# Codebook and quantisation in one block, two thresholds per product over stacked half rows, keys' low parts by a product in the turned keys' bank

## What is computed

```python
lora_delta = lora_B @ lora_A * 0.5                       # 512x64 @ 64x512
cb = codebook / max(max|codebook|, 1e-8)                 # 64 entries, in any order
scale = exp(scale_log)                                   # one per row and group of 128
normalized = (weight + lora_delta) / scale               # 512 x 512
thresholds = (cb[:-1] + cb[1:]) * 0.5                    # 63
idx = searchsorted(thresholds, normalized, side='left')
w = (cb[idx] - normalized) + normalized
w_eff = w * scale + lora_delta
x = x + x @ w_eff.T
```

```python
x = x + attention(x, Wq, Wk, Wv, Wo, norms, k_cache, v_cache, block_table, cache_seqlens)
```

## Time and profile before

| | us |
|---|---|
| median of 3 runs (2248.16 to 2250.21) | 2248.35 |
| the profiled execution | 2244.9 |
| its span in the trace | 2243.0 |

### The profile page before, as it was taken

One profiled execution on the slowest core, in us unless ns is written; L12 is line 12 of the kernel. 1 busy time (PEld: TensorE's weight loads), 2 busy tenths in 40 slices (PEclk: granted clock), 3 DMA queues, 4 the chain that ended last, 5 costly groups with the idle time before them and its releaser, 6 DMA issues.

```text
span 2243.0 us, 61281 instructions
## 1 busy us (share of the span) xinstructions
PE 2158.3 (96%) x18068; PEld 1411.6 (63%) x18068; DVE 1727.7 (77%) x3942; ACT 1465.5 (65%) x4967; POOL 1251.3 (56%) x2067
## 2 busy tenths in 40 slices
PE   5786989999999999999999999999999999999998
PEld 2343556666666666666666666666666666666665
DVE  6995668777777777777777777777777777777785
ACT  2542557676677776676676667667666666666664
POOL 3422126656666655665656666666656566665663
PEclk9997999999999999999999999999999999999999
DMA  3687658667667667667669667666566656666663
GB/s 103 221 279 248 222 167 238 195 193 207 200 194 207 197 191 216 203 198 211 198 191 300 179 189 238 185 177 175 175 188 181 181 173 186 183 178 177 184 178 104
DMA packets 478727, 438.06 MB, mean 195 GB/s; under 512 B 53037, under 2 KB 407676, under 8 KB 477886
## 3 DMA queue, kind: packets, MB, share of 16 engines
q1 hardware_dynamic: 433278, 295.70, 44.7%
q0 software_dynamic: 40960, 134.25, 19.6%
q10 hardware_dynamic: 4160, 4.19, 0.5%
HBM read 377.24 MB, written 56.70 MB: 193 GB/s over the span
## 4 chain that ended last, share of the span: by engine, by line
PE 84%; DVE 1%; issue 0%; ACT 0%; DVEq 0%; ACTq 0%
PE PR L1257 21%; PE Op L1238 15%; PE WOp L1296 15%; PE Sp L1204 15%; PE PTp L1215 11%; PE TRp L1270 3%; PE Sp L1207 1%; PE Op L1220 1%; PE Op L1240 1%; PE TRp L1281 1%; DVE masked L1448 0%; PE WOp L1281 0%; ACT masked L1353 0%; DVE WoT L1507 0%; DVE OT L1466 0%
## 5 line engine op out<-in xcount | busy, mean ns | idle before, releaser
L669 POOL DMA_INDIRECT pages<-values_split,rows x512 | 526.4, 1028 | 104.0 <-issue 78.5
L1347 ACT ACTIVATE pts<-PTp 128x512 f16<-128x512 f32 x512 | 305.7, 597 | 363.9 <-PE PTp L1215 363.8
L1257 PE MATMUL PR<-Wt,xT 128*128 128x512 f16 x2232 | 539.1, 380 | 0.0
L1238 PEld LDWEIGHTS Op<-pts,pages 128*128 128x128 f16 x6144 | 385.4, 98 | 121.1 <-DVE OT L1466 4.2
L1238 PE MATMUL Op<-pts,pages 128*128 128x128 f16 x6144 | 426.6, 219 | 2.4 <-DVE OT L1466 2.3
L1204 PE MATMUL Sp<-pages,qT 128*128 128x512 f16 x1536 | 416.2, 380 | 6.9 <-PEq L184 6.9
L1448 DVE CUSTOM_DVE_ANT_0 masked<-Sp,mask 128x544 f32<-128x544 f32 x512 | 370.0, 723 | 60.4 <-PE Sp L1207 54.3
L1453 DVE TENSOR_TENSOR pts<-PTp,pts 128x512 f16<-128x512 f32 x512 | 351.5, 686 | 75.1 <-ACT pts L1347 74.9
L1353 ACT ACTIVATE masked<-masked,small 128x544 f32<-128x544 f32 x512 | 379.0, 740 | 9.4 <-DVE small L1448 8.5
L1296 PE MATMUL WOp<-WoT,OT 128*128 128x512 f16 x1536 | 377.5, 379 | 0.0
L1466 DVE TENSOR_TENSOR OT<-Op,OT 128x128 f16<-128x128 f32 x512 | 148.2, 289 | 266.3 <-ACT p L1341 262.7
(11 more groups left out here) (211 smaller groups left out, 3075.5 us busy)
## 6 DMA issues: line engine op xcount, KB each, us to landing
pages<-keys_transposed SPq DMA_DIRECT2D x2048, 64.0 KB
mask<-mask_rows SPq DMA_DIRECT2D x128, 128.0 KB
v<-new_values SPq DMA_DIRECT2D x96, 128.0 KB
weights_split<-wdst SPq DMA_DIRECT2D x40, 256.0 KB
keys_transposed<-pages SPq DMA_DIRECT2D x32, 256.0 KB, 3.4
values_split<-pages SPq DMA_DIRECT2D x16, 512.0 KB, 3.6
rope_s<-rope_table SPq DMA_DIRECT2D x32, 256.0 KB
pages<-values_split,rows POOLq DMA_INDIRECT x512
```

The lines of the kernel that those rows point to most:

```text
L669: nc.gpsimd.indirect_dma_start(out=vS[:, n % 2, c, :, :].rearrange("p l n -> p (l n)"), out_offset=None, in_=v_d, in_offset=bass.IndirectO ...
L1238: nc.tensor.matmul(o, vS[:, par, c, low, h * D:(h + 1) * D], pts[:, u % 2, part, c * P:(c + 1) * P], start=(k == 0), stop=False)
L1257: m = nc.tensor.matmul(bank(k), xT[:, c, xl, :], Wp[:, c, wl, GROUP_COL[k]:GROUP_COL[k] + HID], start=(i == 0), stop=(i == NPASS - 1))
L1347: nc.scalar.activation(pts[:, u % 2, 0, :], PTp[:, :], ACT.Copy).then_inc(G.pt_hi, 1)
```

## The change

The codebook block is gone as a block of its own; its work stands at the head of block 2, without a barrier behind it.

- **Order of SP's loads:** codebook, LoRA factors, scale_log, weight, then the first chunk of keys and values, the small tables, chunk 1; then the jump's store and load; then chunk 2 and the page table (`bt_raw`, formerly ahead of the small tables).
- **LoRA:** ScalarE, not VectorE, copies the turned lora_B and the four products. Sum and scaling of `norm` run in quarters of 512 columns.
- **Two thresholds per product:** ScalarE's queue copies rows 0 to 63 of `norm` by two DMAs (512 KB each) into the lower and upper 64 partitions of `pair_rows[0]`, and rows 64 to 127 likewise into `pair_rows[1]`. A comparison (`thr2`) tests 64 rows against an even threshold in partitions 0 to 63 and against the next, odd one in partitions 64 to 127. The weights of a product (`pair_weights`, 32 kept matrices) have 64 columns with the jumps' f16 parts and 64 with their low parts; both thresholds' contributions add up in the product. 64 comparisons (32 per half of the rows) and four f16 products for each.
- **Joining:** after each half ScalarE copies the four banks to SBUF (`sums_out`), high sums in partitions 0 to 63, low sums in 64 to 127; at the end two f32 products per bank with shifted identities (`joined`) add high and low and put both halves of the rows in place.
- **Keys' low parts:** the turned keys stay in their PSUM bank, a product of a negative identity with the f16 high part is added onto them (`rest`), and ScalarE copies the remainder (`keys_low`). The keys' staging has four buffers instead of two. Turns, copies and low parts have new places in the order of steps.
- **GpSimd:** `positions` come before the page table, which is worked through in two parts of 512 numbers after the values' chunks 3 and 8. **Angles:** four steps before the first comparison, four after steps 1 to 7; tables after steps 38 to 52.

The diff, cut to its core:

```diff
+        stacked = sb("stacked", [P, 3 * P // 2], F32)
+        thr2, jump2, jump2_lo = (scr[:, 3264 + 32 * i:3296 + 32 * i] for i in range(3))
+        pair_rows = [acc, wgt]
-        clear()
-        DRING, AHEAD = 8, 5
+        NP = NCB // 2
+        STEPS = 2 * NP
+        RING, AHEAD = 3, 5
...
@ sync
                 load(1)
+                sp.wait_ge(G.sq_done, 1)
+                sp.dma_start(jump_d[0:NCB - 1].rearrange("(n o) -> n o", o=1), tiny[0:63, 8:9]).then_inc(G.jump_moved, 16)
+                sp.wait_ge(G.jump_moved, 16)
+                sp.dma_start(jump[:, 0:NCB - 1], jump_d[0:NCB - 1].rearrange("(o n) -> o n", o=1).to_broadcast([P, NCB - 1])).then_inc(G.jump_moved, 16)
                 load(2)
+                sp.dma_start(bt_raw, page_list.to_broadcast([P, B * NPP])).then_inc(G.pages_loaded, 16)
...
@ tensor
+                def rest(n):
+                    pe.wait_ge(G.kt_hi, n + 1)
+                    nc.tensor.matmul(t_bank[n % 3].rearrange("p (h q n) -> p h q n", h=KVH, q=PPC), negident,
+                                     kst[n % 4][:, :, :, 0, :].rearrange("p q h n -> p h q n"), start=False, stop=True, skip_group_check=True).then_inc(G.kt_rest, 1)
...
+                turn(0)
+                turn(1)
+                turn(2)
+                pe.wait_ge(G.const_done, 3)
+                rest(0)
+                for step in range(STEPS):
+                    phase, j = divmod(step, NP)
+                    pe.wait_ge(G.mask16_done, step + 1)
+                    pe.wait_ge(G.diag_done, 2 * (j + 1) if phase == 0 else 2 * NP)
+                    for k in range(4):
+                        if phase == 1 and j == 0:
+                            pe.wait_ge(G.sums_out, k + 1)
+                        m = nc.tensor.matmul(q_bank[k], pair_weights[j], mask16[step % RING][:, k * 512:(k + 1) * 512], start=(j == 0), stop=(j == NP - 1))
...
+                    if step % 2 == 0 and step // 2 + 1 < NI:
+                        rest(step // 2 + 1)
+                    if step % 2 == 1 and step // 2 + 3 < NI:
+                        turn(step // 2 + 3)
+                for k in range(4):
+                    pe.wait_ge(G.sums_out, 4 + k + 1)
+                    nc.tensor.matmul(q_bank[k], joined[0], sums[0][k], start=True, stop=False)
+                    nc.tensor.matmul(q_bank[k], joined[1], sums[1][k], start=False, stop=True).then_inc(G.bank_joined, 1)
@ scalar
+                def keys_low(n):
+                    a.wait_ge(G.kt_rest, n + 1)
+                    nc.scalar.activation(kst[n % 4][:, :, :, 1, :], t_bank[n % 3].rearrange("p (h q n) -> p q h n", h=KVH, q=PPC), ACT.Copy).then_inc(G.kt_lo, 1)
+                def weights_of_pair(j):
+                    nc.scalar.activation(pair_weights[j][:, 0:P // 2], stacked[:, 0:P // 2], ACT.Copy, scale=jump2[:, j:j + 1]).then_inc(G.diag_done, 1)
+                    nc.scalar.activation(pair_weights[j][:, P // 2:P], stacked[:, 0:P // 2], ACT.Copy, scale=jump2_lo[:, j:j + 1]).then_inc(G.diag_done, 1)
+                a.wait_ge(G.norm_done_first, 1)
+                for phase in range(2):
+                    rows_of = norm[64 * phase:64 * phase + 64, :]
+                    for half in range(2):
+                        a.dma_start(pair_rows[phase][64 * half:64 * half + 64, :], rows_of).then_inc(rows_paired[phase], 16)
...
+                    if step % 2 == 0 and step // 2 + 2 < NI:
+                        keys_high(step // 2 + 2)
+                    if step % 2 == 1 and step // 2 + 1 < NI:
+                        keys_low(step // 2 + 1)
+                    if step % 4 == 1 and step // 4 + 1 < NC:
+                        values_high(step // 4 + 1)
@ vector
-                    V.tensor_scalar(mask16[j % RING], norm, thr[:, j:j + 1], None, ALU.is_gt).then_inc(G.mask16_done, 1)
-                    if j % 2 == 1 and j >= 5:
-                        keys_low((j - 5) // 2)
+                v.wait_ge(G.jump_moved, 32)
...
+                for step in range(4):
+                    angles(step)
+                for step in range(STEPS):
+                    phase, j = divmod(step, NP)
+                    if step >= RING:
+                        v.wait_ge(G.summed, step - RING + 1)
+                    if j == 0:
+                        v.wait_ge(rows_paired[phase], 2 * 16)
+                    V.tensor_scalar(mask16[step % RING], pair_rows[phase], thr2[:, j:j + 1], None, ALU.is_gt).then_inc(G.mask16_done, 1)
@ gpsimd
                 for c in range(NC):
+                    values_low(c)
+                    if c == 3:
+                        g.wait_ge(G.pages_loaded, 16)
+                    if c in (3, 8):
+                        page_table((c - 3) // 5)
```

More of the change, by code:

```diff
@@ L405, in build, with bank_ready @@
         with nc.Block() as block:
+            def bank_ready(phase, k):
+                return (G.pair_sums, 3 * phase + k + 1) if k < 3 else (G.summed, NP * (phase + 1))
             @block.sync
@@ L440, in _ @@
                 for done in kst_stored:
-                    sp.wait_ge(done, 16 * NI // 2)
+                    sp.wait_ge(done, 16 * NI // 4)
                 for done in vst_stored:
@@ L517, in _ @@
+                for j in range(AHEAD):
+                    weights_of_pair(j)
+                for step in range(STEPS):
+                    phase, j = divmod(step, NP)
+                    if phase == 0 and j + AHEAD < NP:
+                        weights_of_pair(j + AHEAD)
+                    if phase == 1 and j == 0:
+                        for k in range(4):
+                            sums_out(0, k)
+                    if step == 36:
                         a.wait_ge(G.abs_done, 1)
+                        a.wait_ge(G.mask16_done, NP)
@@ new lines, in _ @@
+                V.memset(halfpi, float(3.141592653589793 / 2))
+                V.memset(mask[:, :, :], 0.0)
+                V.memset(n5[:, :, :], 0.0)
+                V.memset(jump[:, 63:64], 0.0)
+                V.memset(thr[:, 63:64], BIG)
+                v.wait_ge(G.codebook_loaded, 3 * 16)
+                link(V.tensor_reduce(out=tiny[:, 1:2], in_=cb_raw, op=ALU.max, axis=AX.X, apply_absolute_value=True))
+                link(V.tensor_scalar(tiny[:, 2:3], tiny[:, 1:2], 1e-8, None, ALU.max))
@@ new lines, in _ @@
+                m.then_inc(G.norm_done_first, 1)
+                v.wait_ge(G.jump_moved, 32)
+                V.tensor_copy(jump2[0:64, :], jump[0:64, 0:64:2])
+                link(V.tensor_copy(jump2[64:128, :], jump[64:128, 1:64:2]))
+                link(V.tensor_copy(jump2_hi, jump2))
+                V.tensor_tensor(jump2_lo, jump2, jump2_hi, ALU.subtract).then_inc(G.steps_ready, 1)
+                for step in range(4):
+                    angles(step)
+                for step in range(STEPS):
+                    phase, j = divmod(step, NP)
+                    if step >= RING:
[3 more added lines that the diff above has]
+                    V.tensor_scalar(mask16[step % RING], pair_rows[phase], thr2[:, j:j + 1], None, ALU.is_gt).then_inc(G.mask16_done, 1)
+                    if step in (1, 3, 5, 7):
+                        angles(4 + step // 2)
+                    if 38 <= step <= 52 and step % 2 == 0:
+                        tables((step - 38) // 2)
+                    if step == 54:
@@ new lines, in _ @@
+                link(Q.memset(negident, 0.0))
+                Q.affine_select(out=negident, in_=negident, compare_op=ALU.not_equal, fill=-1.0, base=0,
+                                pattern=[[-1, P]], channel_multiplier=1).then_inc(G.const_done, 1)
+                link(Q.memset(stacked[:, :], 0.0))
+                for i, (c0, first) in enumerate(((0, 0), (0, -64), (P, 0), (P, -64))):
+                    m = Q.affine_select(out=stacked[:, c0:c0 + 64], in_=stacked[:, c0:c0 + 64], compare_op=ALU.not_equal, fill=1.0, base=first,
+                                        pattern=[[-1, 64]], channel_multiplier=1)
+                    if i < 3:
+                        link(m)
+                    else:
+                        m.then_inc(G.const_done, 1)
```

353 lines of the change are left out of this document (154 added, 199 removed).

## The result

| | before | after |
|---|---|---|
| median us (of 4 runs each) | 2248.26 | 2230.59 (2227.97 to 2234.06) |
| ratio, 95% interval | 1 | 0.992 (0.9902 to 0.9938) |
| the profiled execution, its span | 2244.9, 2243.0 | 2227.97, 2226.2 |
| next block starts, in the span | 204.8 | 182.57 |

The kernel became faster by 17.7 us, where 27.6 were forecast. The time lies inside the range of 2207 to 2236, 9.9 us above the forecast of 2220.7 and 2.6 us above the band of 2212 to 2228 that had been given a chance of 0.62.

A forecast was written before the change was run, and what follows sets the result against it. VectorE was taken to bound the quantisation loop, TensorE and transfers close behind. Start 29.5, loop 125.5 and tail 21 put the next block at 177.2 instead of 204.8: 2248.35 - 27.6 = 2220.7 us, range 2207 to 2236.

The forecast's parts named there:

- What bounds the loop: Quantisation loop: VectorE is the fullest engine and sets the pace; TensorE is hidden, 2.5 us against VectorE's 3.9 per two steps.
- rival 4: Quantisation loop: TensorE stays at its lower clock, next block at 209.5, time 2253; chance of slower 0.03.
- The start: Before the loop: pair copies and jump row both ready by 29.5 us for the first comparison, bounds 27 and 33.
- plus 3: Start: 3 us for spreading the jump row over the partitions after its store returns at 18 to 21.
- VectorE's sum: Quantisation loop: VectorE's work, collisions and stalls add up to 125.5 us, ending at 155.0.
- comparisons with collisions and page table: Loop: 64 comparisons at 1.20, 15 GpSimd subtractions costing 1.9 each, and 2 us for the page table.
- angles, tables, mask row: Loop on VectorE: last four angle steps, eight table steps and the mask row, 13.7 us.
- waits: Loop stalls of VectorE: TensorE's lower clock at the start 1.5, change of halves 1, transfers 2; 4.5 us.
- Rival 2: Loop: GpSimd's one-input page table steps exclude comparisons, costing VectorE 16 us instead of 2; time 2235, chance 0.04.
- Rival 1: Loop: transfers become the bound, 36.4 MB taking 138 us; ScalarE waits on stores or loads; time 2232, chance 0.14.
- TensorE, ScalarE, key buffers: Loop: TensorE and ScalarE hidden under VectorE's 3.9 us per two steps; more key staging lets stores queue.
- Tail: From the loop's end to the next block: 20 to 22 us, taken as 21, for 22.2 before.

The follow-up runs named there:

- e3: Kernel after with every product of the quantisation loop issued twice, the second into an unread PSUM bank; ratio to before 0.9939.
- e9: Kernel after with the jump row made by a product and two page table steps after each values' low part from the third chunk; 2211.4 us.
- e11: Kernel after with two staging buffers for turned keys instead of four; ratio to before 1.0015.
- e10: Kernel after with the keys' low parts subtracted by VectorE again, without the `rest` product and its copy; ratio to before 0.9941.
- e12: Kernel after with 14 more waits in GpSimd's queue, after the values' low parts from the third chunk on; 2228.3 us.
- e5: Kernel after with the jump row spread over the partitions by one small product instead of through DRAM; 2224.0 us, ratio to before 0.9882.
- e8: Kernel after with page table before the loop, jump row by a product, and GpSimd's values' low parts cut to one column per half; ratio to before 0.9834.

## Why the prediction was right, and where its steps failed

**What bounds the loop: right.** VectorE is the fullest engine, TensorE is hidden (e3), and rival 4, TensorE at the lower clock, didn't come: 0.91 granted over the loop.

**The start: wrong by 3.5 us.** 29.5 was forecast for the pair copies and 26 to 30 for the jump row. The copies were on time (issued 20.50, landing 8.4 later by the issues' median, so near 29). The jump row was the late one: I took 18 to 21 for the store's return and 3 for the spread; 22.25 and 6.2 were measured. The step that failed most is the term "plus 3": the store had been charged for the traffic in front of it and the reload not.

**VectorE's sum: 129.2 for 125.5.** By its terms, from the rows above:

| term | predicted | measured in after |
|---|---|---|
| comparisons with collisions and page table | 76.8 + 28.5 + 2 = 107.3 | 101.6 |
| angles, tables, mask row | 13.7 | 118.36 - 101.6 = 16.8 |
| waits | 4.5 | 10.8 |

VectorE's work came out near the forecast as a whole: 107.3 + 13.7 = 121.0 forecast, 118.4 measured, and 123.5 in e9, where no wait interrupts it. This is partly luck, since errors of the terms cancel. Comparisons lost 101.6 - 76.8 = 24.8 us to GpSimd, where 30.5 were forecast. With some 0.2 us for each of the page table's 26 steps, 5 to 6 us where I had 2, about 19 are left for the 15 subtractions, 1.3 each and not 1.9. Some subtractions fell on other steps instead, which I had left out (L527, 2.18 us for 1.21; the mask row 2.34 for 0.6), and one ran while VectorE waited. The waits are the step that failed, 10.8 us for 4.5, and they are the page table. I costed its 26 operations by what they do to VectorE and not by what they do to GpSimd, and the prediction names nobody who is queued behind them. The forecast has them at "about 16 us". In the trace they take 39.5 us (16 of 1.53, ten of 1.45 to 1.60), and SP's and TensorE's order carries the delay to VectorE. In the earlier trace rows the number was already there: the GpSimd operation in that row lasted 1.91 us and I read only the comparison beside it.

**Rival 2** (a one-input step of GpSimd excludes a comparison, cited from the Trainium skill, page "SBUF — State Buffer", section "Who interferes with whom") was neither right nor wrong. Beside page table steps two comparisons take 2.86 us:

```profile
109.12 2.86 DVE L618 TENSOR_SCALAR qT<-Wt,WoT 128x2048 f16<-128x2048 f32 x2
109.56 7.74 POOL L705 TENSOR_SCALAR rows<-WoT 32x128 uint32<-32x128 f32 x4
```

Two undisturbed ones take 2.46, so a comparison pays 0.2. The step pays 0.9 (1.48 for 0.61). By the page the later one blocks for all of the other. GpSimd's side is near that; on VectorE's side 0.61 a step was to be lost and 0.2 was.

**Rival 1** (transfers bind, 2232) came near to the time, and the measured time lies in its band of 2228 to 2242, but for another reason. Its signs, ScalarE's waits for stores (30.5 us, where I had wanted under 20) and VectorE's for products, are there, but the DMA engines stood idle in the two stalls. A transfer that is issued late looks in the waits like one that is slow; the 0.00 in the stretch tells them apart.

**TensorE, ScalarE, key buffers: right, with one cover unnamed.** ScalarE was hidden in the kernel after, but by the four key buffers: with two (e11) the loop is 24.6 us longer.

**Where the gain is.** The loop went from 152.3 to 129.2 us and starts 5.5 us later. The 9.2 us for the positions are gone from the waits; the keys' low parts on VectorE would add 8.3 (e10) and eight products per comparison 6.1 (e3). These three add up to about the 23 us of the loop, but no run undoes them together, and the first is read from the waits alone.

**Tail: right but for 0.7 us.** 163.3 to 182.57 are 19.3 us, for 20 to 22 forecast.

**Sum.** Start +3.5, loop +3.7, tail -1.7: the block ends some 5.4 us later than forecast (182.6 for 177.2). The other 4.5 between the block's 22.2 and the medians' 17.7 lie within what the medians can tell (the interval of 0.9902 to 0.9938 is a gain of 14 to 22 us), and e12, which does the same work, gained 20.6.

## What to carry to other kernels

When a step is moved into another engine's queue, price it on both engines, at its duration beside the new neighbours, and then follow the queue: what stands behind it, who waits for that, and with how much slack. A small round trip through DRAM must be priced with the traffic under way, the way back included: the store took 5.9 us beside nothing and 10.6 and 11.7 beside loads, from either queue. A product that spreads the value through PSUM needs no round trip (e5). Two gains need not add: the page table early (6.0 us of the block) and the jump row by a product (3.3) gave 3.4 together, until the page table's work was spread thin (10.6).

## What was new about the hardware

- One-input GpSimd steps of 512 columns last 0.61 us alone and 1.45 to 1.60 beside comparisons, which themselves lose only 0.2.
- A column of 63 numbers needs 5.9 us to DRAM with the DMA engines idle (share 0.03) and 10.6 to 11.7 with loads under way (0.41 and 0.96); its reload, spread over 128 partitions, took 6.2 and 8.6 there.
- With GpSimd's subtractions nearly gone (e8) the transfers of this loop run at a share of 1.02 and 348 GB/s for 80 us: that is where they bind.
- TensorE, ScalarE and VectorE can be idle for about 2 us each at the same place with no releaser in the profile, while GpSimd goes on; what ends it is not known.
